# A ring of gathered rows for eight edge blocks instead of four in a graph network layer

## The reference, cut to what matters

```python
row, col = (edge_index[0], edge_index[1])            # src, dst
msg_in = jnp.concatenate([node_features[row], node_features[col]], axis=-1)
h = jax.nn.relu(msg_in @ Wm1 + bm1)
h = jax.nn.relu(h @ Wm2 + bm2)
messages = h @ Wm3 + bm3
agg = jax.ops.segment_sum(messages, col, num_segments=num_nodes)
...
agg = agg / jnp.clip(count, 1.0)[:, None]
node_in = jnp.concatenate([node_features, agg], axis=-1)
upd = jax.nn.relu(node_in @ Wn1 + bn1) @ Wn2 + bn2
x = _layernorm(x + node_features + upd, axis=-1)
```

## Time and profile before

| | |
|---|---|
| median of 3 runs | 1422.41 us (1417.72 to 1422.87) |
| the profiled execution | 1424.14 us, of which its span is 1422.2 us |
| granted TensorE clock, mean | 0.988 |
| busy: TensorE / its weight loads | 1250.7 / 1170.6 us |
| busy: VectorE, ScalarE, GpSimd | 982.0, 742.4, 793.8 us |

### The profile page before, as it was taken

The page is one execution under the profiler, slowest core; times in us unless marked ns, Lnnn a source line. Parts: engine busy times, 40 slices in busy tenths (PEclk is TensorE's granted clock), DMA queues, the critical chain, the costliest instruction groups (busy, mean ns, idle before and its releaser), DMA issues.

```text
span 1422.2 us, 33710 instructions
## 1 busy us (share of the span) xinstructions
PE 1250.7 (88%) x9586; PEld 1170.6 (82%) x9587; DVE 982.0 (69%) x2072; ACT 742.4 (52%) x1392; POOL 793.8 (56%) x814
## 2 busy tenths in 40 slices
PE   7978888888888888888899889889998899998897
PEld 6868888888888888888888888888898888888686
DVE  6856666666676666676676676777676777777576
ACT  3545555455555555555555555555555555455485
POOL 2166666666666666666666666666666666664000
PEclk9999999999999999999999999999999999999899
DMA  9665555444544554554454555445554444544022
GB/s 308 279 229 153 149 144 147 154 145 143 151 146 143 151 150 142 148 147 142 149 151 139 149 147 145 147 145 144 150 142 146 151 139 146 152 137 135 9 66 87
DMA packets 135604, 211.40 MB, mean 149 GB/s; under 512 B 24247, under 2 KB 102669, under 8 KB 134030
## 3 DMA queue, kind: packets, MB, share of 16 engines
q1 hardware_dynamic: 98030, 108.43, 24.9%
q0 software_dynamic: 37536, 102.55, 24.5%
HBM read 188.09 MB, written 22.80 MB: 148 GB/s over the span
## 4 chain that ended last, share of the span: by engine, by line
PE 83%; issue 11%; DVE 2%; SPq 1%; DMA 1%; ACT 1%; DVEq 0%; ACTq 0%
PE bank L1437 41%; PE bank L1413 12%; PE bank L1324 7%; PE sums L1345 4%; PE sums L1341 4%; PE sums L1347 3%; PE sums L1349 3%; PE bank L1469 2%; PE sums L1482 1%; PE bank L1234 1%; PE bank L1454 1%; PE bank L1219 1%; PE sums L1219 1%; DMA b_win<-b_table 1%; PE sums L1455 0%
## 5 line engine op out<-in xcount | busy, mean ns | idle before, releaser
L630 POOL DMA_INDIRECT a_edge<-a_table,src_idx x782 | 774.4, 990 | 452.3 <-remote 257.7
L1437 PE MATMUL bank<-w,h 128*128 128x256 f32 x4692 | 660.1, 283 | 96.3 <-issue 93.7
L1437 PEld LDWEIGHTS bank<-w,h 128*128 128x128 f32 x4692 | 595.9, 189 | 107.0 <-issue 106.2
L1106 DVE SCALAR_TENSOR_TENSOR h<-bank,h 128x512 fp32r<-128x512 f32 x391 | 269.1, 688 | 338.0 <-issue 328.2
L732 ACT ACTIVATE h<-bank 128x512 fp32r<-128x512 f32 x391 | 234.2, 599 | 478.3 <-remote 435.0
L721 ACT COPY bank<-b_bc 128x512 f32<-128x512 f32 x391 | 231.4, 592 | 112.0 <-issue 62.3
L1413 PE MATMUL bank<-ident,a_edge 128*128 128x128 f32 x1564 | 240.7, 275 | 30.0 <-issue 26.1
L1118 DVE SCALAR_TENSOR_TENSOR h_lo<-bank,h_hi 128x512 fp32r<-128x512 f32 x391 | 266.9, 683 | 0.1
L740 ACT ACTIVATE h_hi<-bank 128x512 fp32r<-128x512 f32 x391 | 233.0, 596 | 2.8 <-PE bank L1437 2.8
L1413 PEld LDWEIGHTS bank<-ident,a_edge 128*128 128x128 f32 x1564 | 181.1, 141 | 56.3 <-issue 50.2
L1324 PE MATMUL bank<-onehot_t,b_win 128*128 128x256 f32 x782 | 189.9, 324 | 0.7 <-issue 0.7
(11 more groups left out here) (186 smaller groups left out, 679.5 us busy)
## 6 DMA issues: line engine op xcount, KB each, us to landing
b_win<-b_table SPq DMA_DIRECT2D x391, 128.0 KB
rel<-rel_dram SPq DMA_DIRECT2D x196, 128.0 KB
a_edge<-a_table,src_idx POOLq DMA_INDIRECT x782
a_table<-work SPq DMA_DIRECT2D x12, 512.0 KB, 4.1
b_table<-work SPq DMA_DIRECT2D x5, 1024.0 KB
b_table<-h SPq DMA_DIRECT2D x4, 1024.0 KB
f_x<-in_x SPq DMA_DIRECT2D x12, 256.0 KB, 4.8
b_table<-a_edge SPq DMA_DIRECT2D x3, 1024.0 KB, 5.4
```

Source lines behind the costliest of these rows:

```text
L630: pool.indirect_dma_start(a_edge[:, b % R * TB + t, :], None, a_table, bass.IndirectOffsetOnAxis(ap=src_idx[:, b * TB + t:b * TB + t + 1], ...
L1106: dve.scalar_tensor_tensor(h1[:, k % U, 1, :], bank[k % 2][:, :], 0.0, h1[:, k % U, 0, :].bitcast(F32), ALU.max, ALU.subtract).then_inc(s_ ...
L1437: ins = pe.matmul(to, h1[:, j, a, h * EB + t * P:h * EB + (t + 1) * P], w2[:, b, h, :], start=False, stop=(a == 1 and h == KH - 1), skip_g ...
```

## The change

`R` becomes 8, so `a_edge` holds the rows of eight blocks. GpSimd waits only ahead of every fourth block, until TensorE has expanded the blocks up to b - 5, and then issues the eight gathers of four blocks. VectorE's wait for the gather is left out but in the first four blocks; SyncE waits for the gather of a block ahead of loading that block's window, so that `s_bw` stands for both. The bodies of TensorE and SyncE take eight blocks, those of ScalarE and VectorE stay at four. `b_win`, `rel` and the one-hot slots keep their sizes. Buffers of the other stages move from `work` into the larger `a_edge`.

```diff
-R = 4
+R = 8
...
-        WORK = 11910
+        WORK = 9872
...
             def body(i):
-                first = load_words(sp, words_sp, i * U, U, PAD_DST)
-                for k in range(U):
-                    if there(i, k - RB):
-                        sp.wait_ge(s_ex, i * U + (k - RB + (2 if k % 2 == 0 else 1)))
+                first = load_words(sp, words_sp, i * R, R, PAD_DST)
+                for k in range(R):
+                    if there(i, k - RB, R):
+                        sp.wait_ge(s_ex, i * R + (k - RB + (2 if k % 2 == 0 else 1)))
...
-                    if there(i, k):
+                    if there(i, k, R):
+                        if not isinstance(i, int) or i > 0 or k >= U:
+                            sp.wait_ge(s_g[k], i * (16 * TB) + 16 * TB)
                         sp.dma_start(b_win[:, k % RB, :].bitcast(F32),
...
             for b in range(NBE):
-                if b >= R:
-                    pool.wait_ge(s_ex, b - R + 1)
+                if b >= R and b % U == 0:
+                    pool.wait_ge(s_ex, b - R + U)
                 for t in range(TB):
                     pool.indirect_dma_start(a_edge[:, b % R * TB + t, :], None, a_table,
...
                 dve.wait_ge(s_bw[k % RB], nth(i, k, 16))
-                dve.wait_ge(s_g[k % R], nth(i, k, 16 * TB))
+                if isinstance(i, int) and U * i + k < U:
+                    dve.wait_ge(s_g[k], 16 * TB)
...
             def body(i):
-                words = load_words(pe, words_pe, i * U, words_of(i, BACK + 1), PE_TOP)
-                for k in steps(i, BACK + 1):
+                words = load_words(pe, words_pe, i * R, len(steps_pe(i)), PE_TOP)
+                for k in steps_pe(i):
                     word = words[k]
...
-            bodies(pe, body)
+            bodies(pe, body, NI_R)
```

More of the change, by code:

```diff
@@ L46, in gnn_layer @@
     NI = NB // U
+    NI_R = NB // R
     PAD_DST = NW * P - 1
@@ L389, in f_out, with bodies, there, among_last @@
             return hx[1][:, g * GW * P:(g * GW + size(g)) * P].rearrange("p (w d) -> p w d", d=D)
-        def bodies(e, body):
+        def bodies(e, body, n=NI):
             body(0)
             body(1)
-            with nc.Fori(2, NI - 1, engines=bass.OrderedEngineSet([e.engine]), head_slot={e.engine: 0}) as i:
+            with nc.Fori(2, n - 1, engines=bass.OrderedEngineSet([e.engine]), head_slot={e.engine: 0}) as i:
                 body(i)
[L396 to L403, removed]
+            body(n - 1)
+        def there(i, k, size=U):
+            return not isinstance(i, int) or 0 <= size * i + k < NBE
+        def among_last(i, k, n, size=U):
+            return isinstance(i, int) and size * i + k >= NBE - n
         def nth_last(i, k, n):
@@ L1384, in expand_and_sum @@
                     expand(b_win[:, k % RB, :], onehot_t[:, k % 2, :], k).then_inc(s_ex, 1)
-                if there(i, k - BACK):
-                    if isinstance(i, int) and U * i + k == BACK:
+                if there(i, k - BACK, R):
+                    if isinstance(i, int) and R * i + k == BACK:
                         pe.wait_ge(s_sz, 1)
-                    if not there(i, k):
-                        pe.wait_ge(s_h2l[(k - BACK) % U], nth(i, k - BACK))
-                    if there(i, k - BACK - 1):
+                    if not there(i, k, R):
+                        pe.wait_ge(s_h2l[(k - BACK) % U], nth_pe(i, k - BACK))
+                    if there(i, k - BACK - 1, R):
                         with pe.If(word > 2**13 - 1):
@@ L1398, in expand_and_sum, with steps_pe, nth_pe @@
                     ins = other_sums(bank_at(own), (k - BACK) % U, k - BACK)
[L1399 removed]
+                    if among_last(i, k - BACK, BACK + 1, R):
                         ins.then_inc(s_sg, 1)
[L1401 removed]
+                elif there(i, k - BACK - 1, R):
                     sum_all_further(k - BACK - 1, word)
+            def steps_pe(i):
+                return range(R + BACK + 1) if isinstance(i, int) and i == NI_R - 1 else range(R)
+            def nth_pe(i, k):
+                return i * (R // U) + k // U + 1
             def body(i):
[L1405 to L1406 removed]
+                words = load_words(pe, words_pe, i * R, len(steps_pe(i)), PE_TOP)
+                for k in steps_pe(i):
                     word = words[k]
[L1408 to L1410 removed]
+                    if there(i, k, R):
+                        pe.wait_ge(s_ot[k % U], nth_pe(i, k))
                         for t in range(TB):
@@ L1416, in body @@
                                                 skip_group_check=True)
-                    if there(i, k) and there(i, k - BACK - 1):
+                    if there(i, k, R) and there(i, k - BACK - 1, R):
                         with pe.If(word > 0):
```

36 lines of the change are left out of this document (20 added, 16 removed).

## The result

The changed kernel takes 1843.97 us (median of 4 runs, 1841.12 to 1846.04), the kernel before 1421.54 us beside it: a ratio of 1.298 (95% interval 1.296 to 1.300). The forecast was 1316 us, with 1240 to 1430 as its range. It is wrong in sign and far outside the range.

A forecast was written before the change was run, and what follows sets the result against it. The prediction took GpSimd's rounds, a run of gathers plus a delayed TensorE count, to bound the kernel. 1424.1 - 109 (waits) + 2 (written-out blocks) = 1317 us, 1316 us as a median; range 1240 to 1430 us.

The forecast's parts named there:

- What bounds the kernel: Edge loop: GpSimd's round of 6.28 us for two blocks sets the pace; 215 us isn't TensorE's own work.
- Rival A: TensorE bounds in its own right, delay from SyncE's pair of loads; only loop ends count, 1408 us; chance 0.20.
- a count that falls into the last two gathers of a run arrives some 2.15 us after the last one's start: TensorE's s_ex counts to GpSimd and ScalarE: run and this 2.15 us delay together make the round pacing everybody.
- rival B: GpSimd's runs of eight: counts held from the third gather on, round of 14.2 us, 1586 us; chance 0.20.
- the benign one: Reading that only counts in a run's last two gathers are held; forecast case, 1300 to 1345 us, chance 0.47.
- Can TensorE follow?: TensorE's four blocks need 10.7 us, under GpSimd's round of 11.4 us, with one stop of about 0.7 us.
- point of decision: GpSimd's round: slower once it passes 12.5 us, that is with holds over about 7 us.
- GpSimd's waits: Idle time ahead of GpSimd's gathers: 96 waits of 1.36 us left, 1117.7 us in all, 109 us less.
- Rival C: TensorE's larger loop body leaves its instruction memory, adding fetches; 1355 to 1460 us; chance 0.06.
- VectorE, SyncE and the loops: VectorE's dropped wait, SyncE's added wait and fewer loop ends each taken as 0; written-out blocks +2 us.
- Rival D: GpSimd's gathers: nothing held any more, 1240 us; chance 0.07.
- The chances: Whole kernel: faster 0.69, within 0.5% 0.09, slower 0.22; 0.78 for the range 1240 to 1430 us.

The follow-up runs named there:

- rows_by_sync: The changed kernel, but from block 4 on SyncE loads consecutive (wrong) rows, same bytes, with plain DMAs in place of GpSimd's gathers; 1211.1 us.
- wait_two: The changed kernel, but GpSimd waits ahead of every second block, so a run has four gathers again; 1405.1 us.
- wait_two_timed: Timed repeat of wait_two, all edits of the change but the run's length; 1423.61 against 1420.62 us before, ratio 1.003.
- plain_rows: The changed kernel with plain GpSimd DMAs of 128 consecutive (wrong) rows, same bytes and places, instead of the indirect gathers; 1211.8 us.

## Why the prediction was wrong, point by point

- **What bounds the kernel: right.** It said that GpSimd's rounds set the pace and that 215 us are not TensorE's own work. Without indirect gathers the kernel takes 1211 to 1212 us, 190 us under the 1401.2 of the kernel before in the set of rows_by_sync. Rival A, a bound of TensorE or of SyncE's pair of loads, falls with rows_by_sync, which keeps both and takes 2.58 us a block.
- **The step that failed: "a count that falls into the last two gathers of a run arrives some 2.15 us after the last one's start".** The size fits a run of four and only that; it was read as a fixed delay behind a run. It is a remainder: a release at some 0.2 + 1.43 us for each gather, against 1.25 us of issue, so 2.14 us behind four, 2.48 behind six, 2.75 behind eight. And in the longer run it isn't the last two gathers' counts that are late: the one at 4.87 us waited till 11.6 us. The rows on record already spoke against the reading: in the run of six the expansion ended at 100.06, with gathers 1.27 us apart in the fourth one and not in the last two (the fifth begins at 100.2), and was heard at 103.89, 2.41 us after the last gather and 8.78 after the first. 0.2 + 6 x 1.43 is 8.78 as well. The text used this row for rival B only, said that all its rows fit both readings, and then gave the benign one 0.47.
- **"Can TensorE follow?": wrong by 6 us a round.** It had 10.7 us of work for four blocks, with one stop of 0.7 us in a round of 11.4; 16.8 us came out. In the 6.3 us after 709.2 TensorE is busy for 3.3, and over the next 4 us its clock is 0.50. The stop of 1.0 us in the earlier trace rows was priced as a constant; the stops in the second layer are 91 us in wait_two with runs of four, 202 with six and 264 with eight.
- **GpSimd's waits: the arithmetic was right and worth nothing.** 96 waits were left, but 673.2 us stand for them in the first fence, 7 us each instead of 1.36.
- **Rival B was the right kind and too small.** It had every count held from the third gather on, and 14.2 us a round, 1586 us. Measured: release at 11.6 (it said 11.2), the next block's expansion 0.7 us later, and then a whole block at the lower clock, 4.3 us, in place of what B had as 2.7 us for both. B left out TensorE's stops and the lower clock behind them. It put its point of decision at holds of over about 7 us; the hold is 6.7 us in the row, and 6.5 to 7.5 in 91 blocks, so even there its sum had a round of 12.5 us where 16.8 was measured. The sign that it named, ScalarE waiting 4 us and more and TensorE idle in several places of a run, did come.
- **Rival C: no.** The body of eight blocks is not fetched anew in the loop; the queue of instructions has 19 fetches, six more than before, for 46 passes, and by the trace none of them between 180 and 1718 us:

```profile
q8 instruction: 19, 0.31, 0.1%
```

- **VectorE, SyncE and the loops at 0 to 2 us: right, taken together**, by wait_two_timed (1.003). Rival D, nothing held, came only where the gathers were spread out or replaced. Its 1240 us is GpSimd's own pace with all gathers back to back, and no kernel shows it.
- **The chances**: by the prediction's own terms faster adds up to 0.70 and within 0.5% to 0.08, where it has 0.69 and 0.09. Nothing rests on that.

What stays open is what the indirect gathers occupy: the runs show the time (1.43 us a gather, whatever the rows or bytes), whom it hits (TensorE's counts and matmuls, register instructions of VectorE) and its steps of 0.7 us, not where it lies. Nor is shown why a spacing of 1.51 us isn't enough, or how much of the 422 us the clock has by itself, beyond the bound of some 300 us: no kernel held the clock up while the runs stayed at eight.

## What to carry to other kernels

A delay that is always seen behind bursts of one length is not a constant: before lengthening the burst, vary its length or its spacing in one run and see whether the delay grows. And redo the claim on every row at hand: a single run of six was enough to refute it here. In this kernel the bursts of four with gaps cost 190 us against none, and bursts of eight 630; the gaps looked like idle time to be removed and kept the loss down. Here waiting for the consumer every two blocks was what kept four gathers apart from the next four.

## What the runs showed of the hardware

- An indirect gather of GpSimd is issued in 1.25 us (1.17 with 32 rows). In runs of 4, 6 and 8 of them the last late count of TensorE is heard 5.90, 8.84 and 11.63 us after the first, 1.43 us a gather, the same within 0.15 us for 96 or 32 rows and for 256 bytes a row. With plain DMAs of GpSimd with the same bytes, one in 0.54 us, no count is late (plain_rows).
- With eight indirect gathers 1.25 us apart, counts of TensorE come up to 7 us late and its own matmuls come singly or in threes and fours, 0.7 or 1.4 us apart. At 1.51 us 46 of 100 counts are still over 2.2 us late; at 1.56 us 1 of 100, at 1.9 and 2.4 us none.
- The granted clock was 1.00 over 5.1 us of full work, 0.82 over the next 6.3 us, in which TensorE was busy for 3.3, and 0.50 (1.2 GHz) over the 4 us behind them, in which it was busy again; twelve matmuls took 1.58 us at 1.00 and 2.77 us at 0.50 for the most part.
